# Post-norm decoder layer on one core: the self-attention's value products regrouped from every fourth step to every eighth

## The reference, cut to what matters

```python
# self-attention: 32 heads of 16 features, 8 batches of 128 tokens
scores = einsum('bqhd,bkhd->bhqk', q, k) * scale + alibi   # causal mask
attn = softmax(scores)
out = einsum('bhqk,bkhd->bqhd', attn, v).reshape(B, S, D)
x = layernorm(x + out @ w_out.T + b_out)
```

## Time and profile before

| | before |
|---|---|
| timed runs, median (range) | 881.51 us (878.49 to 882.42) |
| profiled execution | 878.4 us, span 876.3 us |
| TensorE busy | 854.1 us, 97% of the span |
| VectorE busy | 604.9 us |
| ScalarE busy | 426.1 us |
| GpSimd busy | 454.9 us |
| self-attention, 74.90 to 255.90 us | 181.00 us |
| clock granted to TensorE, mean | 0.995 of full speed |

### The profile page before, as it was taken

The page is one execution under the profiler, slowest core; times in us unless marked ns, Lnnn a source line. Parts: engine busy times, 40 slices in busy tenths (PEclk is TensorE's granted clock), DMA queues, the critical chain, the costliest instruction groups (busy, mean ns, idle before and its releaser), DMA issues.

```text
span 876.3 us, 15306 instructions
## 1 busy us (share of the span) xinstructions
PE 854.1 (97%) x4748; PEld 711.5 (81%) x4748; DVE 604.9 (69%) x2030; ACT 426.1 (49%) x1424; POOL 454.9 (52%) x406
## 2 busy tenths in 40 slices
PE   7999999999999999999999999999999999999996
PEld 6788888788877788888888888888888887778884
DVE  5466888788876776766666667667666667546646
ACT  5336977877853444444444444444444555440320
POOL 4626866766674544444444444444444569455002
PEclk9999999999999999999999999999999999999998
DMA  8679898876762111212113113122120122000001
GB/s 288 259 227 221 216 204 166 175 157 150 199 216 110 49 37 42 103 33 101 36 37 109 37 37 109 37 63 83 37 108 28 58 72 86 22 16 25 25 2 47
DMA packets 68368, 88.23 MB, mean 101 GB/s; under 512 B 7232, under 2 KB 44352, under 8 KB 67264
## 3 DMA queue, kind: packets, MB, share of 16 engines
q1 hardware_dynamic: 68288, 87.26, 35.2%
HBM read 64.13 MB, written 23.07 MB: 100 GB/s over the span
## 4 chain that ended last, share of the span: by engine, by line
PE 85%; DVE 6%; issue 3%; POOL 3%; ACT 2%; DMA 0%; POOLq 0%; DVEq 0%; ACTq 0%
PE banks L35 68%; PE banks L1116 6%; PE banks L1098 3%; PE banks L752 2%; PE banks L770 1%; PE banks L743 1%; DVE B_prob L840 1%; ACT B_prob L681 1%; POOL B_wv L171 1%; PE banks L367 1%; POOL x L114 0%; PE banks L122 0%; POOL D_up L171 0%; PE banks L370 0%; PE banks L371 0%
## 5 line engine op out<-in xcount | busy, mean ns | idle before, releaser
L35 PE MATMUL banks<-C_wo,C_o 128*128 128x512 f32 x768 | 192.3, 399 | 0.7 <-issue 0.5
L35 PE MATMUL banks<-xT,C_w 128*128 128x512 f32 x768 | 185.7, 390 | 0.8 <-DVE xT L137 0.8
L35 PEld LDWEIGHTS banks<-xT,C_w 128*128 128x128 f32 x768 | 143.6, 188 | 31.1 <-issue 1.6
L35 PEld LDWEIGHTS banks<-C_wo,C_o 128*128 128x128 f32 x768 | 139.6, 188 | 28.9 <-issue 1.3
L1057 ACT ACTIVATE C_o<-banks 128x512 fp32r<-128x512 f32 x64 | 38.3, 598 | 227.7 <-PE banks L35 227.7
L681 ACT ACTIVATE B_prob<-B_prob,B_top 128x128 f32<-128x128 f32 x256 | 99.6, 392 | 27.5 <-DVE B_top L840 27.5
L1037 ACT ACTIVATE C_prob<-C_prob,C_top 128x128 f32<-128x128 f32 x256 | 99.1, 391 | 10.2 <-DVE C_top L1182 10.2
L171 POOL TENSOR_TENSOR C_wo<-stage,C_wo 128x512 fp32r<-128x512 f32 x32 | 40.9, 1277 | 110.6 <-ACT C_wo L166 110.6
L171 POOL TENSOR_TENSOR C_w<-stage,C_w 128x512 fp32r<-128x512 f32 x32 | 40.9, 1278 | 101.9 <-ACT C_w L166 101.8
L1244 POOL TENSOR_TENSOR C_q<-C_t,C_t 128x512 f32<-128x512 f32 x64 | 82.9, 1296 | 16.1 <-DVE C_t L1169 16.1
L593 POOL TENSOR_TENSOR B_prob<-B_prob,B_rden 128x512 f32<-128x512 f32 x64 | 67.7, 1058 | 38.4 <-DVE B_rden L849 38.3
(11 more groups left out here) (150 smaller groups left out, 1639.2 us busy)
## 6 DMA issues: line engine op xcount, KB each, us to landing
C_kv<-cross_kv_d SPq DMA_DIRECT2D x8, 1536.0 KB, 7.0
cross_kv_d<-B_v_out SPq DMA_DIRECT2D x16, 512.0 KB, 4.0
stage<-wq_dram SPq DMA_DIRECT2D x32, 256.0 KB, 2.6
stage<-wo_dram SPq DMA_DIRECT2D x32, 256.0 KB, 2.6
heads_q<-heads_q_d SPq DMA_DIRECT2D x96, 64.0 KB, 3.6
heads_k<-heads_k_d SPq DMA_DIRECT2D x96, 64.0 KB, 3.8
heads_q_d<-cT SPq DMA_DIRECT2D x8, 512.0 KB, 2.9
heads_k_d<-cT SPq DMA_DIRECT2D x8, 512.0 KB, 2.8
```

The costliest lines, as they stand in the source:

```text
L35: mm = eng.matmul(out, stationary[i], moving[j], start=first and n == 0, stop=last and n == len(PASSES) - 1)
```

## The change

`weigh` is called in every eighth step (n = 12, 20, ..., 60) for a whole batch (four calls, `C = 4`) in place of every fourth step (n = 8, 12, ..., 60) with two calls. The turned probabilities have nine buffers in place of six, three of them at an address that the cross-attention's first weights use later. So these three weights are split one step later (61, 62, 63), and their high part waits until the batches' products before the last have been made. `turned_slot` numbers the buffers; in the last batch only six are used.

```diff
-    LT, LV, TURNED = 3, 8, 6
+    LT, LV = 3, 12
@@
-    NEXT_SPLIT = {60: 0, 61: 1, 62: 2}
+    NEXT_SPLIT = {61: 0, 62: 1, 63: 2}
@@
-        self.pT = pool("pT", 72, [P, self.TURNED, HG * S])
+        self.pT = [pool(f"pT{i}", kb, [P, HG * S]) for i, kb in enumerate((72, 74, 76, 78, 80, 82, 120, 122, 124))]
@@
+    def turned_slot(self, m):
+        return m % len(self.pT) if m < self.NS - NG else (m - self.NS + NG + 2) % 6
+
+    def wait_turned_free(self, eng, m):
+        held = [i for i in range(m) if self.turned_slot(i) == self.turned_slot(m)]
+        if held:
+            eng.wait_ge(self.s_pv, held[-1] // 2 + 1)
+        elif m >= 6:
+            eng.wait_ge(self.before.s_lo, len(self.before.pieces))
+
     def copy_turned(self, eng, m):
         eng.wait_ge(self.s_tp, m + 1)
-        wait(eng, self.s_pv, (m - self.TURNED) // 2 + 1)
-        eng.activation(self.pT[:, m % self.TURNED, :], self.tp, ACT.Copy).then_inc(self.s_turned[0], 1)
+        self.wait_turned_free(eng, m)
+        eng.activation(self.pT[self.turned_slot(m)][:, :], self.tp, ACT.Copy).then_inc(self.s_turned[0], 1)
@@ def scalar(self, eng, n):
         if n in self.NEXT_SPLIT:
+            eng.wait_ge(self.s_pv, (self.NS - NG) // 2)
             self.cross.piece_hi(eng, self.NEXT_SPLIT[n])
@@ def tensor(self, eng, n):
         self.scores(eng, n)
-        if n >= self.LV and n % 4 == 0:
-            for k in range(2):
+        if n >= self.LV and (n - self.LV) % NG == 0:
+            for k in range(C):
                 self.weigh(eng, (n - self.LV) // 2 + k)
         if n >= self.LT:
             self.transpose(eng, n - self.LT)
@@ def copy_odd(self, eng, m):
         eng.wait_ge(self.s_tp, m + 1)
-        wait(eng, self.s_pv, (m - self.TURNED) // 2 + 1)
-        eng.tensor_copy(self.pT[:, m % self.TURNED, :], self.tp).then_inc(self.s_turned[1], 1)
+        self.wait_turned_free(eng, m)
+        eng.tensor_copy(self.pT[self.turned_slot(m)][:, :], self.tp).then_inc(self.s_turned[1], 1)
```

More of the change, by code:

```diff
@@ L770, in weigh @@
                 mm = eng.matmul(self.ov[b % 2][32 * q:32 * q + 32, c * S:(c + 1) * S], self.v[:, b, at:at + 2 * DH],
-                                self.pT[:, (2 * k + head // HG) % self.TURNED, head % HG * S:(head % HG + 1) * S],
+                                self.pT[self.turned_slot(2 * k + head // HG)][:, head % HG * S:(head % HG + 1) * S],
                                 start=second == 0, stop=second == 1)
```

## The result

| | before | after |
|---|---|---|
| timed runs, median (range) | 878.12 us (876.26 to 882.42, 11 runs) | 885.62 us (881.76 to 886.85, 11 runs) |
| ratio of times | | 1.0075, 95% interval 1.0061 to 1.0089 |
| profiled execution | 878.4 us, span 876.3 us | 885.59 us, span 883.5 us |
| self-attention | 181.00 us | 186.45 us |
| clock granted to TensorE, mean | 0.995 | 0.993 |

The change makes the kernel 6.6 us slower by the ratio (0.0075 x 878), 7.5 us by the medians. Forecast were 4.8 us more, 886.3 us. The three runs of before from which that median was reckoned lay high: their median was 881.51 us, that of eleven runs 878.12.

The account below looks back on a forecast made before the run. TensorE's list was taken to pace self-attention, with VectorE nearly full in steps 16 to 19. Batches summed 3.4 + 0.5 + 0.9 = +4.8 us: 883.2 us profiled, 881.5 + 4.8 = 886.3 us median, range 879.5 to 890 us.

Parts of the forecast that it names:

- A burst: Weighing on TensorE: 0.44 us per call plus 0.28 us once per burst; removing two calls saves 1.16, lengthening adds 0.88.
- Rival 4: Weighing bursts: extra calls cost more than 0.44 us each, 7 x 0.28 on top, 888.3 us; chance 0.05.
- Step 17: After the removed burst of step 16, transposes wait 0.76 us for VectorE's copy of group 13, which doesn't move.
- Rival 1: The saving stays because VectorE and ScalarE work earlier too: -2.0 us, 879.5 us; chance 0.12.
- Steps 18 and 19: Transposes in step 18 in time by 0.1 us; in step 19 a 0.2 us stall for VectorE's copy of group 15.
- Batches 16, 24, 40, 48, 56: Five like batches in self-attention: -1.16 + 0.96 + 0.88 = +0.68 us each, 3.4 us together.
- rival 2: VectorE runs earlier in some batches and step 32 gives back a part: +1 us, 882.5 us; chance 0.14.
- Step 8: First removed burst: stalls for GpSimd's key weights and copies in steps 8, 9 and 11, 0.8 us; batch +0.5 us.
- Step 32: Whole 1.16 us lost waiting for value weights in steps 34 and 35, step 36 adds 0.88: +0.9 us.
- Rival 3: Long burst delays VectorE into steps 13, 21 and so on, 0.4 to 0.6 us a batch: +8.3 us, 889.8 us; chance 0.09.
- The other edits: Nine buffers, the later split of `C_w`, and loads for step 12: priced at nothing.
- Idle time of TensorE: In self-attention, rises from 2.3 to about 9 us, the stage from 181.0 to about 185.8 us.

Follow-up runs that it names:

- experiment 6: High parts of the value weights of steps 34 and 35, and two low parts, split ahead in steps 32 and 33: kernel before 877.33 us, changed kernel 881.76 us.
- experiment 1: Changed kernel with `weigh` called as before (two calls every fourth step), keeping nine buffers and the later weight split: 878.91 us, ratio 1.0001.
- experiment 4: Changed kernel with the row's statistics moved from step 15 to step 20, later root, normalising and turning, row transposes in their own bank: 877.43 us, ratio 0.999.
- experiment 5: Changed kernel with the row's statistics moved behind VectorE's copy in step 16, still one bank for turned probabilities: 880.53 us, ratio 1.0026.
- experiment 8: Changed kernel repeated, 884.8 us; kernel before with 24 extra matmuls in step 60, 883.58 us; changed kernel with 12 extra, 886.12 us; executions also compared by mean clock.
- experiment 7: Changed kernel with both late row statistics and early value weights, timed twice: 876.39 us, ratio 0.9979, and 875.81 us, ratio 0.998.
- before delayed: Kernel before with 24 extra, overwritten matmuls in step 60, nothing moved: 883.58 us, ratio 1.0062.
- experiment 3: Changed kernel with a second PSUM bank for turned probabilities, the weighed values having one bank: 881.45 us, ratio 1.0028.
- after again: Changed kernel timed and profiled once more, unchanged: 884.8 us, ratio 1.0065.
- after delayed: Changed kernel with 12 extra, overwritten matmuls in step 60: 886.12 us, ratio 1.0079.
- experiment 2: Changed kernel with each four-call burst divided: one call in steps with n mod 8 = 0, three in those with n mod 8 = 4: 881.2 us, ratio 1.0023.

## Why the prediction was right

Its mechanism was right, and the batches of the stage came out to a tenth of a microsecond; of the batch at step 32 it had the sum and not the place, and what the timed runs show beyond the stage it did not have.

- *A burst.* Forecast: the long one about 1.96 us; 1.95 us. Step 20 grows by 0.88: 4.09 - 3.22 = 0.87 us. Each call costs 0.44 again. Rival 4 is out.
- *Step 17.* A wait of 0.76 us forecast, with the copy as releaser: the step lasts 2.84 us against 2.07, 0.77 us. The copy was to be independent of TensorE; it lies at 116.90 - 114.65 = 2.25 us behind the start of step 16, as before (115.55 - 113.30). Rival 1 asked for a copy that moves, and is out.
- *Steps 18 and 19.* None and 0.2 us forecast; none and 0.19 us.
- *Batches 16, 24, 40, 48, 56.* +0.68 us forecast, +0.68 to 0.69 measured (steps 16 to 21: 1.35 to 2.03). Steps 16 to 19 last 9.68 us, 9.65 forecast. No batch loses less than the others, so rival 2 is out.
- *Step 8.* Waits of 0.5, 0.1 and 0.2 us in steps 8, 9 and 11 forecast, 0.6, none and 0.18 measured; the batch costs 1.33 - 0.85 = +0.48 us, against +0.5. TensorE's filler waits for the key weights:

```profile
93.66 1.64 PE L35 MATMUL banks<-cT,B_wk 128*128 128x512 f32 x6 [0.35 <-POOL B_wk L171]
```

- *Step 32.* +0.9 us forecast, 3.56 - 2.70 = +0.86 measured, but for a reason that was only half right. I had put the whole loss on the value weights, with steps 34 and 35 waiting 1.2 us longer in sum. Of 1.14 us lost, 0.77 are the copy's wait in step 33, as in all batches, and only 0.36 are in step 34, where the transposes wait for ScalarE:

```profile
166.41 0.63 PE L767 MATMUL banks<-ident,B_prob 128*128 128x128 f32 x4 [0.77 <-ACT B_pT L667]
```

Step 35 is unchanged. That the sum was right is in part luck. Either cause takes the whole lead: with early weights (experiment 6) the changed kernel still loses 0.77 us in step 33, and in step 34 waits for VectorE's value split.
- *Rival 3* (it goes on into the next steps): step 21 lasts 2.07 us, as before. VectorE has caught up by then.
- *The other edits.* Nothing forecast, nothing measured (experiment 1).
- *Idle time of TensorE.* 9 us forecast, 6.9 measured by the table. The stage lasts 186.45 us for 185.8 forecast, and the excess is the 0.68 us that came in steps 3 and 4. But the table counts less idle than there is: in step 17 it shows 0.59 us for a start that is 0.75 us late, since the end of the matmuls before it is drawn later than the start of the next ones can be.

The step that was missing is the one from the stage to the end. I took it that every microsecond of the stage arrives at the end unchanged and nothing is added. In the profiled execution 1.6 us are added at 296 us by a lower clock, and the executions' clocks show that this is not rare. The 0.7 us of steps 3 and 4 come before anything that the change touches, and are within what the profiles of the other kernels differ by up to step 8.

The base was the other error: three runs of before with a median of 881.5 us. The predicted time of 886.3 us is close to 885.6 us by luck, because a base that was 3.4 us too high and an increase that was 1.8 to 2.7 us too small nearly cancel.

The cause, as the runs show it: taking a burst out of TensorE's list brings 1.16 us only where the other engines are ahead of it. In step 17 VectorE's copy was 0.76 us too late for that, behind the statistics (experiments 4 and 5), and the copy in step 19 another 0.2. The one way in and out of the narrow form that a batch saves, 0.28 us, cannot pay 0.96 us of waiting. That accounts for the 4.8 us of the stage. What the timed runs show beyond that, 1.8 us by the ratio, goes at least in part with the clock (1.6 us in the profiled execution, 1.1 us by the means of experiment 8); why the clock was lower stays open.

## What to carry to other kernels

Work that paces an engine may cover a backlog of another one elsewhere: before it is moved, look for the copy that frees a single buffer behind it, and read how long before its use it is ready; with less slack than the moved work is long, the rest of the saving is a wait. If a move fails for that, move the other engine's backlog to where the work now stands (here the statistics into the long burst): that took the loss away, and left a gain in the stage that the timed runs of experiments 4 and 7 show barely or not at all. Take the base from more than three executions, and compare executions at like clocks where an increase is a few microseconds.

## What the runs showed of the hardware

- Behind an idle time of TensorE of 1.94 to 1.98 us, at the same place of the program, twelve matmuls took 2.90 to 2.92 us in seven of the fourteen profiles (before, before delayed, experiments 3 and 4, the changed kernel of 6, both of 7). In the seven others (after, after again and after delayed, experiments 1, 2 and 5, the kernel before of 6) they took 3.95 to 4.50 us, at a granted clock of 0.66 to 0.87 over the 5 us stretch, so partly at the lower level. The lower clock goes neither with the changed stage nor with the moment.
- A second place lies later. Before the change it is at 785 us, with a granted clock of 0.67; after the change it is at 790 us, with 0.71. TensorE is not idle ahead of it; it makes sixteen small products. The lower clock came there in seven of the fourteen profiles too (before, after, after again, experiments 3 and 4, the changed kernel of 6, the first of 7). The profiles with neither place (before delayed and the second of 7) have a mean clock of 0.997, those with one 0.994 or 0.995, those with both (after, twice) 0.993; that of experiment 3, also 0.993, has the lower clock once more, behind its wait in step 34. Executions at a mean of 0.993 took 3.9 to 4.3 us more than those at 0.997, of before and of after alike.

```profile
782.32 1.95 PE L1522 MATMUL banks<-D_fold,D_gT 16*128 16x8 f32 x16
```

```profile
785.00:790.00 5.00, 5.00 (x16) 3.93 (x16) 2.14 (x11) 0.69 (x1) 5.00 (x5) 0.67 0.00 0
```

- Transposes that wait for VectorE's copy start 0.14 to 0.15 us after the copy has ended: 117.56 to 117.71 and 121.89 to 122.03 after the change, as 250.23 to 250.38 in the earlier trace rows.
- A burst of products in the narrow form costs 0.44 us for each call of two groups of heads, and 0.28 us once: its records last 0.65 us for one call, 1.08 for two, 1.52 for three (experiment 2) and 1.95 for four.
